# Rotated Q and K parts in places of their own, three stores per block, loads on two queues, and a written-out order of TensorE's steady stages

## The reference

```python
Q, K, V = x @ qw, x @ kw, x @ vw              # 16 heads of 8
Q, K = rope(Q, freq), rope(K, freq)           # pairs (2i, 2i+1) turned by cos, sin
score = einsum('bhqd,bhkd->bhqk', Q, K) / sqrt(8) - 1e10 * (1 - causal)
weights = softmax(score - max(score))
attn = einsum('bhqk,bhkd->bhqd', weights, V)
x = layernorm(x + merged(attn) @ ow)
gates = top-2 of softmax(x @ router_w + router_b) over 4 experts
x = layernorm(x + sum_e gates_e * ((silu(x @ w1_e) * (x @ w3_e)) @ w2_e))
```

## Time and profile before

| | |
|---|---|
| median of the runs | 496.91 us |
| the profiled execution's own time | 497.89 us |
| its span | 496.2 us |
| granted TensorE clock, mean | 0.924 of full speed |
| prologue, to the first T | 0 to 85.6 us |
| seven steady stages (first S to first S) | 87.8 to 306 us, 31.2 us each |
| last stage and experts | from 306 us |

### The profile page before, as it was taken

One profiled execution on the slowest core, in us unless ns is written; L12 is line 12 of the kernel. 1 busy time (PEld: TensorE's weight loads), 2 busy tenths in 40 slices (PEclk: granted clock), 3 DMA queues, 4 the chain that ended last, 5 costly groups with the idle time before them and its releaser, 6 DMA issues.

```text
span 496.2 us, 7475 instructions
## 1 busy us (share of the span) xinstructions
PE 416.2 (84%) x2397; PEld 209.4 (42%) x2420; DVE 313.3 (63%) x1027; ACT 267.1 (54%) x377; POOL 190.2 (38%) x255
## 2 busy tenths in 40 slices
PE   5715473899898998989989888989999999999992
PEld 2302310222223222232222322327888788788781
DVE  3526374687887878878778786333556756765844
ACT  1220300557556576575755757676665575565560
POOL 3631320205215152151431513224565574665662
PEclk9957555799999999999999999889999999999996
DMA  6644544021122121221212100000000000000000
GB/s 230 190 125 120 159 100 122 13 63 47 20 65 50 47 61 24 65 49 40 60 33 64 41 3 0 3 0 1 2 0 2 21 1 1 22 1 2 22 0 21
DMA packets 46198, 23.47 MB, mean 47 GB/s; under 512 B 30320, under 2 KB 43248, under 8 KB 46160
## 3 DMA queue, kind: packets, MB, share of 16 engines
q1 hardware_dynamic: 46160, 23.00, 17.6%
HBM read 14.21 MB, written 8.59 MB: 46 GB/s over the span
## 4 chain that ended last, share of the span: by engine, by line
PE 58%; DVE 17%; SPq 7%; DMA 6%; ACT 5%; issue 4%; POOL 2%; POOLq 0%; DVEq 0%; ACTq 0%
PE o_bank L1055 12%; PE t_bank L1123 8%; PE bank L1123 8%; PE t_bank L1134 8%; DVE maxima L789 7%; PE t_bank L1038 6%; PE bank L1015 6%; PE small_bank L1015 3%; DMA q_op<-max_rows 3%; SPq L408 3%; DVE mg_w L785 2%; DVE mg_t L785 2%; DVE x_w L785 2%; SPq L367 2%; ACT num L628 2%
## 5 line engine op out<-in xcount | busy, mean ns | idle before, releaser
L628 ACT ACTIVATE num<-t_bank 128x1024 f32<-128x1024 f32 (+2 forms) x160 | 145.1, 939 | 110.1 <-PE t_bank L1038 108.8
L549 POOL TENSOR_TENSOR hid_lo<-num,q_op 128x512 fp32r<-128x512 f32 x64 | 83.0, 1300 | 60.9 <-ACT q_op L684 59.7
L518 POOL TENSOR_SCALAR_AFFINE_SELECT num<-num 128x512 f32<-128x512 f32 x64 | 40.3, 636 | 145.6 <-ACT num L628 145.5
L1015 PE MATMUL bank<-k_op,q_op 128*128 128x512 bf16 (+7 forms) x241 | 74.4, 338 | 22.8 <-DMA k_op<-k_scratch 10.8
L1055 PE MATMUL o_bank<-num,v_op 128*32 128x512 f32 (+3 forms) x768 | 84.5, 513 | 1.1
L1038 PE MATMUL t_bank<-q_op,k_op 64*128 64x512 bf16 (+3 forms) x384 | 59.8, 339 | 11.9 <-DMA q_op<-max_rows 10.2
L684 ACT ACTIVATE q_op<-num 128x512 fp32r<-128x512 f32 x64 | 40.5, 632 | 45.1 <-DVE num L916 44.7
L789 DVE TENSOR_REDUCE maxima<-bank 128x1 f32<-128x512 f32 x85 | 58.4, 688 | 7.9 <-PE bank L1015 4.5
L785 DVE CUSTOM_DVE_ANT_0 mg_t<-bank,resid 128x320 f32<-128x320 f32 (+6 forms) x85 | 37.9, 446 | 23.2 <-PE bank L1015 14.4
L1015 PEld LDWEIGHTS bank<-k_op,q_op 128*128 128x128 bf16 x255 | 23.2, 98 | 67.3 <-DVE maxima L789 20.8
L1038 PEld LDWEIGHTS t_bank<-q_op,k_op 64*128 64x128 bf16 x384 | 16.0, 93 | 76.6 <-issue 46.3
(11 more groups left out here) (132 smaller groups left out, 640.8 us busy)
## 6 DMA issues: line engine op xcount, KB each, us to landing
k_op<-k_scratch SPq DMA_DIRECT2D x32, 128.0 KB, 2.3
q_op<-q_scratch SPq DMA_DIRECT2D x64, 51.0 KB
q_scratch<-rope_part SPq DMA_DIRECT2D x24, 128.0 KB, 2.4
k_scratch<-rope_part SPq DMA_DIRECT2D x24, 128.0 KB, 2.4
w_raw<-in_w_all SPq DMA_DIRECT2D x6, 512.0 KB, 4.1
xT<-in_x_feat SPq DMA_DIRECT2D x4, 256.0 KB, 5.4
k_scratch<-k_op SPq DMA_DIRECT2D x4, 256.0 KB
q_op<-max_rows SPq DMA_DIRECT2D x64, 3.0 KB
```

Source lines behind the costliest of these rows:

```text
L518: pool.affine_select(out=tile, in_=tile, compare_op=ALU.is_ge, fill=0.0, base=0, pattern=[[0, GH], [1, P]], channel_multiplier=-1)\
L549: pool.tensor_tensor(hid_lo[:, m % HB, :], hid[:, m % HB, :], hid_hi[:, m % HB, :].bitcast(F32), ALU.subtract).then_inc(f_lo, 1)
L628: act.activation(num[:, t % PB, :, off:CH].rearrange("p (k i) t -> p i k t", i=2)[:, :, h:h + each, :], t_bank[k % TB][:, :, 0:each * (CH ...
L1015: pe.matmul(ring(s, step)[:, 0:width], q_op[u][:, pr, j, :, :].rearrange("p i q -> p (i q)"), k_op[u][:, pr, lo:lo + width], start=True, s ...
```

## The change

The diff does five things.

1. `rope_part` lies in the buffer `num` (free until the first exponential) and has a place for each of the 8 blocks. The waits of ScalarE and GpSimd on `parts_stored` inside the rotation go; ScalarE waits for all stores once, ahead of its first stage.
2. The scratch tensors are laid out as feature, product, token. The products are renumbered so that a part's copies are evenly spaced, and one DMA stores a part to all its copies (a source that repeats): three DMAs per block in place of six. The rows of zeros and of ones leave the scratch tensors: ones are set in both `k_op` (GpSimd memsets, the second pair moved behind the last `third_part`), zeros are kept in a small tensor `zeros`.
3. `load_q` is four DMAs of 48 partitions and, for groups above 1, four more of 3 partitions of zeros. `load_k` is four DMAs of 48 partitions in place of two of 128.
4. The first chunk's K and half of its Q are loaded from ScalarE's queue, in its step n = 4; `parts_stored` counts per chunk.
5. The steady plan is read from a string instead of worked out.

```diff
-Q_PART = (0, 0, 1, 1, 2, 0)
-K_PART = (0, 1, 0, 1, 0, 2)
 PARTS = 3
-KROWS = len(Q_PART) * DH
+PRODUCTS = 6
+Q_AT = ((2, 5, 1), (1, 6, 4), (0, 1, 1))
+K_AT = ((0, 3, 1), (3, 6, 2), (4, 5, 1))
...
+STEADY_ORDER = ("ssssstmsstsssttssspsssttnspstsssppsstsstsspsstsspssttsspsmsttsspssttsspsssttpssnttpp")
+def steady_plan(order):
...
-STEADY = stage_plan(True, True)
+STEADY = steady_plan(STEADY_ORDER)
...
+        q_dram = nc.dram_tensor("q_scratch", (B * H * DH, PRODUCTS, S), BF16).ap()
+        k_dram = nc.dram_tensor("k_scratch", (B * H * DH, PRODUCTS, S), BF16).ap()
+        z_dram = nc.dram_tensor("zeros", (PARTS, S), BF16).ap()
...
+        rope_part = num[:, 0:PB - 1, :, :].rearrange("p i h t -> p (i h t)").bitcast(BF16)\
+            .rearrange("p (n r t) -> p n r t", n=2 * CHUNKS, r=PARTS)
...
+        def load_q(eng, n, u, c, heads):
+            for h in heads:
+                pr, i = divmod(h, 2)
+                at = (n * GH + h) * DH
+                eng.dma_start(q_op[u][i * HR:i * HR + KROWS, pr, c * NB:(c + 1) * NB, i, :],
+                              q_dram[at:at + DH, :, c * CH:(c + 1) * CH].rearrange("d r t -> (d r) t"))\
+                    .then_inc(q_loaded[u][c], 16)
+                if n > 1:
+                    eng.dma_start(q_op[u][i * HR + KROWS:i * HR + QROWS, pr, c * NB:(c + 1) * NB, i, :],
+                                  z_dram[:, c * CH:(c + 1) * CH]).then_inc(q_loaded[u][c], 16)
+        def load_k(eng, n, u, c):
+            for h in range(GH):
+                pr, i = divmod(h, 2)
+                at = (n * GH + h) * DH
+                eng.dma_start(k_op[u][i * HR:i * HR + KROWS, pr, c * CH:(c + 1) * CH],
+                              k_dram[at:at + DH, :, c * CH:(c + 1) * CH].rearrange("d r t -> (d r) t"))\
+                    .then_inc(k_loaded[u][c], 16)
...
-                for part in range(PARTS):
+                for part, (first, end, step) in enumerate((Q_AT, K_AT)[is_k]):
+                    copies = len(range(first, end, step))
                     sp.wait_ge(part_ready[part], n + 1)
-                    for r, of in enumerate(K_PART if is_k else Q_PART):
-                        if of == part:
-                            sp.dma_start(dram[heads, r * DH:(r + 1) * DH, cols], rope_part[part][:, n % 2, :])\
-                                .then_inc(parts_stored[n % 2], 16)
+                    sp.dma_start(dram[b * P:(b + 1) * P, first:end:step, c * CH:(c + 1) * CH],
+                                 rope_part[:, n, part, :].unsqueeze(1).broadcast_to([P, copies, CH]))\
+                        .then_inc(parts_stored[ch], 16)
...
+            for n in range(3):
+                store(n)
+            sp.wait_ge(parts_stored[0], 2 * PARTS * 16)
+            load_q(sp, 0, 0, 0, range(2))
+            for n in range(3, 2 * NC):
+                store(n)
+            sp.wait_ge(parts_stored[1], 2 * PARTS * 16)
+            load_q(sp, 0, 0, 1, range(GH))
+            load_k(sp, 0, 0, 1)
             for n in range(2 * NC, 2 * CHUNKS):
                 store(n)
-            sp.wait_ge(ops_filled, 3)
+            sp.wait_ge(ops_filled, 4)
...
-                if n == 1:
-                    pool.memset(q_flat[1][:, :].bitcast(F32), 0.0).then_inc(ops_filled, 1)
             for n in range(2 * CHUNKS - 2, 2 * CHUNKS):
                 third_part(n)
+            pool.memset(q_flat[1][:, :].bitcast(F32), 0.0).then_inc(ops_filled, 1)
+            pool.memset(k_op[1][:, :, :], 1.0).then_inc(ops_filled, 1)
...
-                if n >= 2:
-                    act.wait_ge(parts_stored[n % 2], STORES * 16 * (n // 2))
-                act.activation(rope_part[0][:, n % 2, :], roped[:, n % 2, :], ACT.Copy).then_inc(part_ready[0], 1)
+                act.activation(rope_part[:, n, 0, :], roped[:, n % 2, :], ACT.Copy).then_inc(part_ready[0], 1)
                 if n >= 1:
                     second_part(n - 1)
+                if n == 4:
+                    act.wait_ge(parts_stored[0], 2 * PARTS * 16)
+                    act.wait_ge(ops_filled, 2)
+                    load_k(act, 0, 0, 0)
+                    load_q(act, 0, 0, 0, range(2, GH))
...
+            for ch in range(CHUNKS):
+                act.wait_ge(parts_stored[ch], 2 * PARTS * 16)
```

More of the change, by code:

```diff
@@ L370, in stored @@
-            def stored(chunks):
-                for i in range(2):
-                    sp.wait_ge(parts_stored[i], STORES * 16 * chunks)
-            for n in range(2 * NC):
-                store(n)
-                if n == 2 * NC - 2:
-                    sp.wait_ge(zeros_stored, 16 * (1 + B * H // ones))
-                    stored(1)
-                    load_q(0, 0, 0)
-                    load_k(0, 0, 0)
-            stored(NC)
-            load_q(0, 0, 1)
-            load_k(0, 0, 1)
+                    sp.dma_start(dram[b * P:(b + 1) * P, first:end:step, c * CH:(c + 1) * CH],
+                                 rope_part[:, n, part, :].unsqueeze(1).broadcast_to([P, copies, CH]))\
+                        .then_inc(parts_stored[ch], 16)
@@ L388, in _ @@
             for c in range(NC):
-                load_q(1, 1, c)
-                load_k(1, 1, c)
-            stored(CHUNKS)
+                load_q(sp, 1, 1, c, range(GH))
+                load_k(sp, 1, 1, c)
+            for ch in range(NC, CHUNKS):
+                sp.wait_ge(parts_stored[ch], 2 * PARTS * 16)
+            sp.wait_ge(zeros_stored, 16)
             for dst, src in ((wo[:, :], ow), (rw[:, :], router_w),
@@ L423, in stage @@
                         sp.wait_ge(t_ready, NT * n + NT)
-                        load_q(s + 1, v, 1)
-                        load_k(s + 1, v, 1)
+                        load_q(sp, s + 1, v, 1, range(GH))
+                        load_k(sp, s + 1, v, 1)
             for s, plan in enumerate(STAGES):
```

70 lines of the change are left out of this document (34 added, 36 removed).

## The result

| | before | after |
|---|---|---|
| median (lowest to highest of 4 runs) | 497.62 us (495.39 to 498.48) | 473.38 us (471.28 to 476.43) |
| profiled execution, its span | 497.89, 496.2 | 471.28, 469.4 |
| mean granted clock | 0.924 | 0.926 |
| first S of the first steady stage | 87.8 | 71.0 |
| first T of the last stage | 307.2 | 282.1 |

The ratio is 0.952 (95% interval 0.946 to 0.959). The forecast was 473.0, and 474.1 for an execution like the profiled one. The forecast had 13, 9.8 and 1.

What follows compares the result with a forecast made beforehand. It took SyncE's queue and store waits to bound the prologue, and 4.5 us of TensorE waiting per steady stage. 497.9 - 13 (prologue) - 10.8 (stages) = 474.1, median 473; range 462 to 488.

Steps and rivals of the forecast that it cites:

- Prologue: Up to the first T: without waits on stores in the rotation, blocks come faster and T starts at 72.5, 13 us earlier.
- `load_q` at 0.6: SyncE's queue: issuing a 48-partition `load_q` was taken as 0.6 us, like a store, within bounds 0.43 and 1.24.
- The last is not decoding but traffic: SyncE's queue: the old `load_q` issue of 1.24 us is set by data draining through a quarter of the DMA engines.
- removed waits: Prologue rotation: without waits on stores, gaps are 3.7 us per block instead of 4.8 to 11.
- Steady stages: Seven stages between prologue and last stage: each takes 29.8 us instead of 31.2, together 9.8 us less.
- The walk: Step-by-step timing of the new steady plan: T(1,0) at 7.7 us, then 20.6 and 1.5 to the stage's end.
- that is hidden in the wait for the rows: Start of a steady stage: some 2 us of slip from late `w_raw` costs nothing unless the `max_rows` rows come early.
- real waiting: Old steady stage: 4.5 us in which TensorE waits for a job bank, VectorE or `max_rows`.
- stages keep their length: Steady stages: stalls move and the clock falls, costing some 1.5 us per stage and the stages' gain; 484 us, chance 0.22.
- Better: Steady stages: rows ready at 6.4 and `w_raw` early enough make a stage 28.5 us; total 465, chance 0.15.
- Slower: SyncE's queue: each DMA costs its issue whatever it moves, END is 10 us, a stage 32.9; total 501, chance 0.10.
- prologue unchanged: Prologue: stores with a repeating source run at under half the present rate, so only the stages gain; 485 us, chance 0.08.

Runs made afterwards that it cites:

- e5: Kernel before, old order and layout, each `load_q` split into a DMA of 48 rows and one of 3: 487.68 us.
- e12: Changed kernel with the removed waits of ScalarE and GpSimd on the stores of block n-2 put back: 475.79 us.
- e4: Changed kernel with one letter of the plan string moved, so MROWS(0) comes 15 places earlier, right behind PV(1,0): 450.06 us.
- e1: Changed kernel with the steady plan worked out as before, so everything of the change but the new order: 480.79 us.
- e10: Changed kernel with `load_k` and the load of `w_raw` swapped at T(1,4), so `w_raw` is issued 1.8 us earlier: 456.3 us.
- e3: Changed kernel with the load of `w_raw` issued at T(1,0), behind `load_q`, instead of at T(1,4): 452.43 us.
- e6: Changed kernel with six store DMAs per block again, one per copy, instead of merged stores: 476.08 us.

## Why the prediction was right, and where its steps were not

- **Prologue: right in its chain, each link a little early.** First S 33 forecast, 32.2 measured; part 2 of block 7 ends at 51.8 and 49.9; MROWS 57.8 and 55.7; first T 72.5 and 70.0. The gain was 15.5 us to the first T instead of 13; the other 1.3 of the 16.8 come from the plan, in which the first S now follows the first T by 0.97 us and not by 2.25. The blocks do come every 3.8 us (3.7 in the sum). The K memset, which had no row, takes 1.80 (1.9 in the sum).
- **`load_q` at 0.6: too high.** The term was mis-sized, and below its own lower bound: 0.30, where the bounds were 0.43 and 1.24. The bound was the shortest issue of the earlier trace rows, and nothing excluded a shorter one. Group 1's 16 loads took 7.7 us (53.45 to 61.15) instead of 8.5, and END's twelve issues 5.0 instead of 7.0. The zeros took 0.35 where 0.64 was taken and 0.47 was the lower bound. "The last is not decoding but traffic" agrees with e5, in which the same bytes in 48 and 3 rows are issued in half the time; what in the 51 rows holds the queue, no run shows directly.
- **What each part of the prologue is worth: not seen.** The text put the gain on the removed waits first. e5 and e12 say otherwise: the 48-row shape brings the first T of the kernel before 7.1 us earlier, while the waits, put back, cost some 2 us and six stores no more than the spread. Taken one at a time these leave 5 to 6 of the 15.5 us open; whether that is what they do for one another, or `load_k` in four pieces and the order of loads and stores, was not tried.
- **Steady stages: 29.8 forecast, 30.6 measured, by errors that cancel.** The walk had T(1,0) at 7.7 us, held by the rows, and 22.1 behind it (20.6 and 1.5 for an S followed by another kind). Measured, in the stage from 190.36: T(1,0) at 9.3, 20.9 behind it. With the first stage, which has no `w_hi` and takes 27.6, the seven gained 8.3 us instead of 9.8. The wait for `w_raw` was forecast to the mechanism and nearly to the size (2 us; 2.6 measured), with its place in the queue and TensorE reaching T(1,0) late. The step that failed is "that is hidden in the wait for the rows". Without the stall the rows are there at about 6 (e4: T(1,0) at 6.1 with 0.37 of wait), below the bound of 6.4, since END is short; so there was 0.4 us of cover for a stall of 2.0. The prediction said that the stall uncovers itself in that case, and it did. The rest of the way to 9.3 is mostly the low clock between T(0,1) and T(1,0), which the sum did not have.
- **The order itself: worth three times what the sum had.** Without the wait a stage takes 26.7 instead of e1's 30.9, 4.2 us less; the sum had 1.4, with the new wait at nothing. The walk's 29.8 is 3.1 above e4's 26.7: 1.7 of it is T(1,0) at 7.7 and not at 6.0, the rest the 22.1 behind it, where e4 needs 20.75. The 0.1 us for an S followed by another kind does show: in e4, behind T(1,0), fourteen S of 512 columns followed by a T or PV take 0.31 us each, those followed by an S 0.22. So it is the walk's 20.6 that was some 1.3 too long. The prediction's own count of TensorE's work without waiting, 24.7 and 2, is 26.7, which is e4's stage: the order, with its wait taken away, removes 4.2 of the 4.5 us that were "real waiting".
- **The rival "stages keep their length" was half right.** It named small S, a stall behind `w_hi`, and the clock at 0.50 behind them, and that is what the stretches show. Its 1.5 us of low clock per stage is within the 1 to 1.7 read above. It was wrong that this takes the whole gain: the order had more to give than was known. Its chance was put at 0.22, and its mechanism occurred in each of six stages; the forecast had taken the clock as unchanged because today's small gaps never moved it. A gap of 2.0 us did.
- **"Better" (465)** would have come with the wait gone: e10, e3 and e4 lie beyond it, at 456 to 450. Its stage of 28.5 was bounded from below by END at 6.4 and the same 22.1; measured, 6.1 and 20.75.
- **"Slower" (queue)** and **"prologue unchanged"**: the queue got shorter by more than forecast, and with stores from a repeating source the first T comes no later than with six single ones (70.03 and 71.51, e6).

So the total is right, with the prologue's gain 3.8 larger and that of the seven stages 1.5 smaller than forecast, and in the stages a larger gain and an unbooked loss. That the median lies within 0.4 us is luck: the profiled execution is 2.8 under its forecast of 474.1, and the median lies 2.1 above that execution where 1.0 below was taken. An engineer who stopped at "473, as forecast" would have left 23 us behind, in a wait that the prediction itself had written down and booked at nothing.

## What to carry to other kernels

When a step is moved, each DMA that follows it in a queue's program moves too: book the new wait at its full size unless a row shows the cover, and work out the cover at its cheap end, not at the likely one. Measure the halves of a change one by one; if they don't add up, look for the wait that one half creates and the other lengthens. Look at what one issue of a load costs before adding loads: here one of 51 rows took 1.24 us, and the same bytes as 48 and 3 rows took 0.31 and 0.34.
